# Layer 0 attention: one merged order of score jobs, value rounds and filling jobs within a step

## The reference, cut to what matters

```python
# hidden_states (2, 1024, 128); 16 query heads, 4 key/value heads, head size 64
q = (hidden_states @ Wq.T).reshape(B, S, 16, 64).transpose(0, 2, 1, 3)
k = (hidden_states @ Wk.T).reshape(B, S, 4, 64).transpose(0, 2, 1, 3)
v = (hidden_states @ Wv.T).reshape(B, S, 4, 64).transpose(0, 2, 1, 3)
k = jnp.repeat(k, 4, axis=1); v = jnp.repeat(v, 4, axis=1)
scores = jnp.einsum('bhqd,bhkd->bhqk', q, k) * 64 ** -0.5
scores = scores + causal[None, None]
probs = jax.nn.softmax(scores, axis=-1)
out = jnp.einsum('bhqk,bhkd->bhqd', probs, v)
return out.transpose(0, 2, 1, 3).reshape(B, S, 1024) @ Wo.T
```

## Time and profile before

| | before |
|---|---|
| median of three runs | 1543.96 us |
| the three runs | 1538.16, 1543.96, 1883.71 us |
| span of the profiled execution | 1535.8 us |
| TensorE busy with matmuls | 1313.7 us, 86% of the span |
| VectorE busy | 976.1 us, 64% |
| ScalarE busy | 692.4 us, 45% |
| GpSimd busy | 115.2 us, 7% |
| attention of layer 0 | about 38 to 668 us of the span |

### The profile page before, as it was taken

The page is one execution under the profiler, slowest core; times in us unless marked ns, Lnnn a source line. Parts: engine busy times, 40 slices in busy tenths (PEclk is TensorE's granted clock), DMA queues, the critical chain, the costliest instruction groups (busy, mean ns, idle before and its releaser), DMA issues. The chain is left out here.

```text
span 1535.8 us, 21410 instructions
## 1 busy us (share of the span) xinstructions
PE 1313.7 (86%) x7772; PEld 774.5 (50%) x7772; DVE 976.1 (64%) x1750; ACT 692.4 (45%) x1319; POOL 115.2 (7%) x155
## 2 busy tenths in 40 slices
PE   4688999999999999966999996526898888789998
PEld 3344444454545454444888874413343333256886
DVE  4455464545555454146999985756777666257998
ACT  2232334342424252433666665421566556525664
POOL 0000000000000000000000000120211111020000
PEclk9698999999999999987999998855899989868998
DMA  3101111120201020104576640022222210102220
GB/s 103 40 15 34 29 34 34 33 48 15 48 19 43 15 43 15 30 0 96 130 159 146 150 92 1 1 35 90 56 55 57 47 47 20 43 21 78 76 103 28
DMA packets 51476, 81.61 MB, mean 53 GB/s; under 512 B 16749, under 2 KB 34453, under 8 KB 47445
## 3 DMA queue, kind: packets, MB, share of 16 engines
q1 hardware_dynamic: 51004, 79.40, 21.1%
q10 hardware_dynamic: 384, 1.05, 0.6%
HBM read 63.75 MB, written 5.68 MB: 45 GB/s over the span
## 5 line engine op out<-in xcount | busy, mean ns | idle before, releaser
L621 DVE TENSOR_REDUCE mraw<-ps 128x1 f32<-128x512 f32 (+3 forms) x304 | 192.7, 659 | 131.1 <-PE ps L507 74.0
L1329 PE MATMUL ps<-qA 128*128 128x512 f32 x960 | 252.9, 400 | 15.2 <-POOL qA L1439 10.6
L723 ACT ACTIVATE shared<-ps 128x512 f32<-128x512 f32 (+1 forms) x216 | 119.4, 567 | 263.3 <-PE ps L540 261.9
L1046 DVE TENSOR_REDUCE mraw<-ps 128x2 f32<-128x1024 f32 (+3 forms) x160 | 173.7, 1114 | 67.6 <-PE ps L954 46.1
L1329 PEld LDWEIGHTS ps<-qA 128*128 128x128 f32 x960 | 182.1, 192 | 64.2 <-POOL qA L1439 12.3
L1101 ACT ACTIVATE shared<-ps 128x512 f32<-128x512 f32 (+2 forms) x320 | 154.4, 561 | 124.7 <-PE ps L970 124.4
L539 PE MATMUL ps<-qA,kH 128*128 128x512 f32 (+3 forms) x384 | 167.8, 447 | 5.8 <-DMA qB<-mT 5.8
L501 PE MATMUL ps<-kH,qA 128*128 128x512 f32 (+3 forms) x384 | 138.8, 415 | 34.9 <-DVE qA L611 18.8
L1393 ACT CAST qA<-shared 128x512 fp32r<-128x512 f32 x160 | 99.3, 621 | 90.4 <-DVE shared L1531 88.9
L1341 PE MATMUL ps<-qA,kH 128*128 128x512 f32 x480 | 136.3, 393 | 4.1 <-DVE qA L1455 4.1
L540 PE MATMUL ps<-qB,kL 65*128 65x512 f32 (+3 forms) x384 | 132.8, 356 | 0.0
(11 more groups left out here) (247 smaller groups left out, 1747.1 us busy)
## 6 DMA issues: line engine op xcount, KB each, us to landing
shared<-comb SPq DMA_DIRECT2D x92, 256.0 KB, 4.3
qB<-qA SPq DMA_DIRECT2D x16, 512.0 KB, 4.8
rB<-a0rec_dram SPq DMA_DIRECT2D x60, 128.0 KB, 2.9
shared<-comb SPq DMA_DIRECT2D x7, 1024.0 KB, 4.4
rB<-a1rec_dram SPq DMA_DIRECT2D x28, 128.0 KB, 2.6
e0wUp<-in_w SPq DMA_DIRECT2D x48, 64.0 KB, 4.6
qA<-q_split SPq DMA_DIRECT2D x24, 128.0 KB
q_split<-qA SPq DMA_DIRECT2D x4, 512.0 KB
```

The lines of the kernel that those rows point to most:

```text
L621: nc.vector.tensor_reduce(out[:, h0:h0 + n_h, qt % 4], src, AX, ALU.max).then_inc(w_free, 1)
L723: nc.scalar.activation(probs(n)[:, hs[0]:hs[-1] + 1, lo:512], src, ACT.Exp, scale=scale)\
L1046: nc.vector.tensor_reduce(out[:, :, js[0]:js[-1] + 1, qt % 4], src, AX, ALU.max).then_inc(x_free, 1)
L1329: ins = nc.tensor.matmul(bank[0:M, :], w[par][:, at:at + M], h[:, cols], start=(r == 0), stop=(r == 2))
```

## The change

`parts` is replaced by `woven_step`. It gives each score job of a step a place between 0 and 1 (four jobs: 1/8, 3/8, 5/8, 7/8), and the three rounds of the unit two steps back the places 1/3, 2/3 and 1. It sorts them, and deals the filling jobs among them evenly by the number of columns that TensorE streams. `values` now issues one round per call; the wait for the probabilities stands before the first round only, and of the two waits for copied accumulators the first round keeps ScalarE's and the others have VectorE's. ScalarE walks the same merged list. The jobs, their order among themselves, the matmuls and the buffers stay the same. VectorE, GpSimd and SyncE keep their order.

```diff
-    def parts(n):
+    def woven_step(n):
+        main = []
+        if n < STEPS:
+            w = 512 - unit_lo(n)
+            jobs = score_jobs(n)
+            main += [((2 * i + 1) / (2 * len(jobs)), "score", i, 2 * w * len(hs)) for i, hs in enumerate(jobs)]
+        if n >= LAG:
+            w = 512 - unit_lo(n - LAG)
+            main += [((p + 1) / 3, "values", p, 4 * w) for p in range(3)]
         fills = due.get(n, [])
-        size = -(-len(fills) // len(heads))
-        return [(hs, fills[size * i:size * (i + 1)]) for i, hs in enumerate(heads)]
+        whole = sum(m[3] for m in main)
+        out, at, done = [], 0, 0
+        for _, kind, i, cost in sorted(main):
+            out.append((kind, i))
+            done += cost
+            while at < len(fills) and (2 * at + 1) * whole <= 2 * len(fills) * done:
+                out.append(("job", fills[at]))
+                at += 1
+        return out + [("job", idx) for idx in fills[at:]]
...
-                def values(n):
+                def values(n, p):
...
-                    if on_diagonal(n):
+                    if p == 0 and on_diagonal(n):
                         pe.wait_ge(masked, diagonals[n + 1])
-                    else:
+                    elif p == 0:
                         pe.wait_ge(p_done, first_score[n + 1])
                     if kt == 0 and n:
-                        pe.wait_ge(o_act, 2 * g + qc)
-                        pe.wait_ge(o_dve, 2 * g + qc)
+                        pe.wait_ge(o_dve if p else o_act, 2 * g + qc)
...
                 for n in range(STEPS + LAG):
-                    for at, (hs, fills) in enumerate(parts(n)):
-                        if hs:
-                            scores(n, first_score[n] + at, hs)
-                        for idx in fills:
-                            job(idx)
-                    if n >= LAG:
-                        values(n - LAG)
+                    for kind, i in woven_step(n):
+                        if kind == "score":
+                            scores(n, first_score[n] + i, score_jobs(n)[i])
+                        elif kind == "values":
+                            values(n - LAG, i)
+                        else:
+                            job(i)
```

More of the change, by code:

```diff
@@ L442, in stage_attention64 @@
         highs.append(highs[-1] + (job[0] == "proj"))
-    def parts(n):
-        heads = score_jobs(n) if n < STEPS else [()]
-        fills = due.get(n, [])
-        size = -(-len(fills) // len(heads))
-        return [(hs, fills[size * i:size * (i + 1)]) for i, hs in enumerate(heads)]
+    def woven_step(n):
[7 more added lines that the diff above has]
+            main += [((p + 1) / 3, "values", p, 4 * w) for p in range(3)]
+        fills = due.get(n, [])
+        whole = sum(m[3] for m in main)
[7 more added lines that the diff above has]
+        return out + [("job", idx) for idx in fills[at:]]
     with ExitStack() as c:
@@ L542, in scores @@
                     ins.then_inc(s_full, 1)
-                def values(n):
+                def values(n, p):
                     g, (qc, kt) = n // NU, UNITS[n % NU]
                     kv, b = divmod(g, B)
-                    if on_diagonal(n):
+                    if p == 0 and on_diagonal(n):
                         pe.wait_ge(masked, diagonals[n + 1])
-                    else:
+                    elif p == 0:
                         pe.wait_ge(p_done, first_score[n + 1])
                     if kt == 0 and n:
-                        pe.wait_ge(o_act, 2 * g + qc)
-                        pe.wait_ge(o_dve, 2 * g + qc)
+                        pe.wait_ge(o_dve if p else o_act, 2 * g + qc)
                     lo = unit_lo(n)
                     first, last = kt == 0, closes(n)
-                    for p in range(2):
+                    if p < 2:
                         for i in range(2):
@@ L564, in values @@
                                                  skip_group_check=True)
[L565 to L568, removed]
+                    else:
+                        for h in range(REP):
+                            ins = nc.tensor.matmul(SUMS[CT * h:CT * (h + 1), lo:512], k.ones[:, 0:CT],
+                                                   probs(n)[:, h, lo:512], start=first, stop=last,
+                                                   skip_group_check=True)
+                        ins.then_inc(pv_done, 1)
                 for idx in due[-1]:
@@ L716, in _ @@
                         act.wait_ge(pv_done, n - RING + 1)
-                    for at, (hs, fills) in enumerate(parts(n)):
-                        if hs:
+                    for kind, i in woven_step(n):
+                        if kind == "score":
                             lo = unit_lo(n)
-                            s = first_score[n] + at
+                            s, hs = first_score[n] + i, score_jobs(n)[i]
                             act.wait_ge(s_full, s + 1)
@@ L724, in _ @@
                                 .then_inc(p_done, 1)
-                        for idx in fills:
-                            if JOBS[idx][0] == "proj":
-                                high(idx)
+                        elif kind == "job" and JOBS[i][0] == "proj":
+                            high(i)
                 act.wait_ge(pv_done, STEPS)
```

## The result

| | before | after |
|---|---|---|
| median | 1541.06 us (4 runs) | 1567.96 us (4 runs, 1564.2 to 1570.04) |
| span of the profiled execution | 1535.8 us | 1565.8 us |

The ratio of the changed kernel to the one before is 1.0193, with a 95% interval from 1.0164 to 1.0221. The ratio goes by the three runs before that lie together (their median is 1538.16 us) and leaves out the fourth, at 1883.71 us. The changed kernel is slower beyond the scatter, by just under 2%, and the interval reaches over 2%. The forecast was 1546 us with a range of 1516 to 1575: the sign and the range hold, but about 5 us were forecast, and 27 came by the medians of the table, 30 by the spans.

A forecast was written before the change was run, and what follows sets the result against it. TensorE was taken to bound layer 0's attention; 35 + 11 us won against 46.5 + 4 lost made it 4.5 us slower, a 1540 us span, put at 1546 us, range 1516 to 1575.

The forecast's parts named there:

- The price of a passage: TensorE getting in and out of rounds: 0.30 us each, 263 instead of 94, 46.5 us lost after 4.2 off.
- The rival by which a passage costs 0.46 us: Every passage between rounds and other work drains TensorE's array: 36 us net lost, 1578 us; chance 0.10.
- The waits for reductions: TensorE's maxima waiting for VectorE's reductions: 35 us won, ends 10 and 50 us.
- the weight loads' waits would fall below 10 us: Sign in the changed profile: the maxima's weight loads wait under 10 us for reductions, down from 50.0 us.
- The waits for projections: TensorE waiting for projection banks to be emptied: 0.9 and 1.1 us a group instead of 2.1, nothing won.
- The clock: Half-clock stretches behind projection waits: five short ones go, the long one's loss halves; 11 us won, between 0 and 13.6.
- The copies out: First and second rounds of a block waiting for ScalarE's and VectorE's copies: 4 us lost, between 0 and 7.
- The passages were not covered: Faster rival: the 0.12 us restart after rounds vanishes, a passage costs 0.18 us; 34 us won, 1508 us; chance 0.09.
- the waits did not simply stay: Slower rival: VectorE's reductions stay late, only 10.3 us dry time goes, clock stays; 40 us lost, 1582 us; chance 0.06.
- the slower rivals: Passages drain the array, 1578 us, chance 0.10; or VectorE's reductions stay late, 1582 us, chance 0.06.
- the forecast span of 1540 us: Profiled execution's span of 1535.8 us plus 4.5 us; the forecast time of 1546 us lies above it.
- 30 won: Slower end of the sum: 51 + 7 us lost and 30 won, 28 us slower.

The follow-up runs named there:

- e2: Changed kernel with three PSUM banks for filling jobs and two for scores; 1528.96 us, ratio 0.9966 to the kernel before.
- e4: Kernel before, order unchanged, with three PSUM banks for filling jobs and two for scores; 1501.34 us, ratio 0.9795.
- e1: Changed kernel with VectorE's normalisation of a group's second block and its output projection one step later; 1543.85 us, ratio 1.0056 to the kernel before.
- e7: e4 with a step's projections behind its other filling jobs where no maximum of theirs is in the step; 1491.11 us, ratio 0.969 to the kernel before.
- e6: Kernel before with the same later normalisation as e1; 1544.17 us, ratio 1.0033.
- e3: Changed kernel with the three rounds together again in mid-step, filling jobs dealt evenly behind the score jobs; 1547.85 us, ratio 1.0092 to the kernel before.
- e5: Changed kernel with rounds still split, but filling jobs in equal portions behind score jobs as before; 1559.95 us, ratio 1.0119 to the kernel before.

## Why the prediction was right and wrong

**The price of a passage: right.** The last group has 18 more passages and almost no waits; I forecast 18 x 0.30 = 5.4 us, and it takes 56.7 instead of 51.3 us. e2 against e4 gives 0.29 us each over the whole stage. The row of passages in the table rose by 37.4 us, where 46.5 had been forecast, but that row also loses the getting going after the stalls that vanished; how much, the table can't tell. The rival by which a passage costs 0.46 us is refuted. The Trainium skill, TensorEngine Tiling (Array Packing), section on tiling modes, says that a change of tiling mode drains TensorE; here both ways and the restart together cost 0.30 us, and no row shows whether the array is empty in between.

**The waits for reductions: about right in size, wrong in the view that was to show it.** They fell by 27.0 us start to start (35 were forecast, with the getting going). Passages and reductions together, the firmer figure, were forecast at 46.5 - 35 = 11.5 us lost, and 37.4 - 27.0 = 10.4 came. The matmuls' dry time fell from 10.3 to 5.1 us. But I had written that the weight loads' waits would fall below 10 us, and they rose from 50.0 to 84.5:

```profile
PE ps L515 <- DVE mraw L636: 5.1, 9, 0.8
```

```profile
PEld ps L515 <- DVE mraw L636: 84.5, 108, 1.4
```

Of these 108 waits 86, with 72.0 us, stand directly behind a round, and the matmul that follows stands dry behind none of the 86. The load stands idle while the round streams, and the view puts that down to the last semaphore. Here a weight load's idle time was no price; I had only taken it as an upper end, and it was a poor one.

**The waits for projections: right.** Two of 0.9 and 1.1 us were forecast in place of 2.1; 0.86 and 1.16 came, and the sum moved from 13.2 to 12.9 us.

**The clock: wrong, and this is the step that failed.** The term "11 us won, between 0 and 13.6" came out at 13.1 us lost, 24 us off, nearly the whole miss. I reasoned that a wait cut in two would leave the clock alone. That was so for the two halves (e1), but I left out what stands behind the projection in VectorE's queue: the normalisation at the head of the next step. It delays one more reduction, a third wait follows within 2 us of the second, and six groups lose the clock for 6.8 us each, 3.4 us a group. With the normalisation moved (e1) the half-clock loss is 4.5 us, 9.2 less than in the kernel before, where 11 had been forecast, and the kernel is 0.6% or 9 us slower than before. So the late reduction accounts for 26.8 - 4.5 = 22.3 us of the term's miss. Queues that the change doesn't touch have to be read at the new place of the work too.

**The copies out: right.** 4 us were forecast with ends at 0 and 7; 2.6 came. A wait of 3.9 us for the rows of the first group's maxima, 2.2 us more than before by the sum of starts, was not foreseen.

**The rivals.** The passages were not covered, and the waits did not simply stay. The measured time lies between the forecast and the slower rivals, by a mechanism that none of them named. That it lies in the range owes something to luck. The forecast time stands 6 us above the forecast span of 1540 us, while the runs of the changed kernel lie only some 2 us above theirs, so the span missed by 26 us and the time by 22. And the "30 won" in the sum's slower end was not worked out: with the ends given before it, 10 us of reductions and nothing for the clock, that end would have been 48 us slower.

## What to carry to other kernels

A finer interleave pays for each switch between column tiles and the full array. Count the switches and price them from one row where the engine passes from one to the other; here 169 more at about 0.30 us ate what the waits gave back. Waits for a buffer were cheaper to remove with one more buffer, taken from a user that could spare it (e4), or by putting the job with the long way home just before a long piece of other work (e7), than by spacing everything out. And when waits are moved, read the queue of the engine that is waited for at the new place: in the changed kernel and in e6 it was one normalisation in front of one reduction that made a new wait, and the clock fell with it.

## What was not expected of the hardware

In the changed kernel three short dry times of TensorE, 0.67, 0.97 and 0.76 us within 9 us, went with 6.8 us at the 1.2 GHz level in each of six groups; the clock fell during the third. With the first two alone (e1: 0.67 and 0.96 us) it stayed at 1.00. No single long idle stretch was needed. But dry time alone doesn't tell when the clock falls, as the same six groups show in one profiled execution of each kernel:

| run | dry times over 0.5 us in each group | groups in which the clock fell |
|---|---|---|
| before | 1.91 | 5 |
| e4 | 1.68 | 3 |
| e6 | 1.91, and 12 us later 1.44 | 1 behind the first, 6 behind the second |
| e3 | 1.97, 1.45 and 0.82 within 15 us, and 25 us later 1.09 | 1 |
| e5 | 1.21 | 1 |
| changed | 0.67, 0.97, 0.76 | 6 |
| e1 | 0.67, 0.96 | 0 |

What else decides stays open.
